# Cross attention of a decoder block on one core: context rows and value-output matrix in high and low parts, the mean row multiplied once per batch

## What is computed

```python
n_q, n_kv = 256, 120
mask = (arange(n_kv)[None, :] % n_q) == arange(n_q)[:, None]   # key j only for query j
sim = where(mask, q @ k.T * scale, -max_float)
out = softmax(sim) @ v
x = layernorm(x + out @ Wout + bout)
```

## Time and profile before

| what | before |
|---|---|
| median of three runs | 1065.95 us |
| the profiled execution | 1066.43 us |
| its span in the trace | 1064.4 us |
| TensorE (PE) busy | 983.4 us, 92% |
| VectorE (DVE) busy | 673.8 us, 63% |
| ScalarE (ACT) busy | 561.9 us, 53% |
| GpSimd (POOL) busy | 481.3 us, 45% |
| TensorE's granted clock, mean | 0.978 of full |

### The profile page before, as it was taken

One profiled execution on the slowest core, in us unless ns is written; L12 is line 12 of the kernel. 1 busy time (PEld: TensorE's weight loads), 2 busy tenths in 40 slices (PEclk: granted clock), 3 DMA queues, 4 the chain that ended last, 5 costly groups with the idle time before them and its releaser, 6 DMA issues.

```text
span 1064.4 us, 22474 instructions
## 1 busy us (share of the span) xinstructions
PE 983.4 (92%) x8461; PEld 840.3 (79%) x8461; DVE 673.8 (63%) x1454; ACT 561.9 (53%) x1338; POOL 481.3 (45%) x378
## 2 busy tenths in 40 slices
PE   3587999999999999999999999999999989989997
PEld 3465888888878888887888888888887759887887
DVE  2547676676867667686776768676432766657543
ACT  1426675766666576666657666665624433335210
POOL 7216455527835552784455278452416220006441
PEclk9668999999999999999999999999999999999999
DMA  6201000000300000030000002001135563640001
GB/s 189 81 1 40 2 12 6 2 17 1 120 4 6 11 2 16 2 120 3 2 16 2 16 2 80 2 6 42 29 98 141 148 158 93 145 99 1 20 20 41
DMA packets 71547, 47.71 MB, mean 45 GB/s; under 512 B 44464, under 2 KB 68112, under 8 KB 71440
## 3 DMA queue, kind: packets, MB, share of 16 engines
q1 hardware_dynamic: 71439, 46.27, 15.9%
HBM read 44.16 MB, written 2.10 MB: 43 GB/s over the span
## 4 chain that ended last, share of the span: by engine, by line
PE 73%; DVE 8%; SPq 8%; issue 5%; ACT 3%; POOL 2%; DMA 1%; POOLq 0%; DVEq 0%; ACTq 0%
PE F L1238 17%; PE F L1098 15%; PE A L1098 15%; PE A L1483 4%; PE A L1185 4%; PE A L1143 3%; PE A L1111 2%; SPq L298 2%; PE A L1202 2%; PE F L1111 2%; ACT prob L919 2%; SPq L306 1%; SPq L308 1%; PE A L1138 1%; PE A L1456 1%
## 5 line engine op out<-in xcount | busy, mean ns | idle before, releaser
L1098 PE MATMUL F<-xt,w 128*128 128x512 f32 x864 | 219.8, 403 | 4.6 <-ACT scratch L1081 3.9
L1098 PEld LDWEIGHTS F<-xt,w 128*128 128x128 f32 x864 | 158.8, 189 | 45.8 <-ACT scratch L1081 7.0
L385 POOL TENSOR_TENSOR ht<-scratch,ht 128x512 fp32r<-128x512 f32 x128 | 173.1, 1368 | 45.4 <-ACT ht L951 42.9
L1238 PE MATMUL F<-w,ht 128*128 128x256 f32 x1536 | 189.3, 282 | 2.0 <-POOL ht L385 2.0
L1238 PEld LDWEIGHTS F<-w,ht 128*128 128x128 f32 x1536 | 182.7, 188 | 7.8 <-issue 4.6
L374 POOL TENSOR_TENSOR rstd<-var,minus_half 128x4 f32<-128x4 f32 x32 | 37.6, 1174 | 225.4 <-DVE var L501 225.4
L948 ACT ACTIVATE scratch<-F,b_now 128x512 f32<-128x512 f32 x128 | 87.7, 685 | 44.4 <-PE F L1098 29.4
L1098 PE MATMUL A<-wa,xt 128*128 128x512 f32 x384 | 94.4, 402 | 3.5 <-issue 3.2
L1098 PEld LDWEIGHTS A<-wa,xt 128*128 128x128 f32 x384 | 72.4, 192 | 20.6 <-issue 3.6
L380 POOL TENSOR_TENSOR x<-x,vec_f 128x1024 f32<-128x1024 f32 x16 | 37.9, 2369 | 105.1 <-DVE scratch L514 105.1
L951 ACT ACTIVATE ht<-scratch 128x512 fp32r<-128x512 f32 x128 | 80.9, 632 | 4.1
(11 more groups left out here) (204 smaller groups left out, 2010.9 us busy)
## 6 DMA issues: line engine op xcount, KB each, us to landing
raw_f<-in_L_attn_W_dram SPq DMA_DIRECT2D x8, 1024.0 KB, 5.6
scratch<-in_L_ffn_fc_B_dram SPq DMA_DIRECT2D x32, 256.0 KB, 3.6
scratch<-in_L_ffn_fc_A_dram SPq DMA_DIRECT2D x32, 256.0 KB, 3.5
x<-in_x_dram SPq DMA_DIRECT2D x4, 512.0 KB, 7.4
raw_f<-in_L_ffn_fc_A_dram SPq DMA_DIRECT2D x32, 64.0 KB, 2.4
scratch<-in_x_dram SPq DMA_DIRECT2D x1, 2048.0 KB, 9.2
raw_f<-in_L_ffn_fc_B_dram SPq DMA_DIRECT2D x32, 64.0 KB, 3.0
out_dram<-x SPq DMA_DIRECT2D x3, 512.0 KB, 2.9
```

Source lines behind the costliest of these rows:

```text
L385: pool.tensor_tensor(ht[:, 1, m, :], hf[:, m % 2, :], ht[:, 0, m, :].bitcast(F32), ALU.subtract).then_inc(h_lo, 1)
L1098: last = pe.matmul(out, lhs(a, c), rhs(b, c), start=k == 0, stop=k == len(total) - 1)
L1238: last = pe.matmul(F[:, t % 2, 0:D], ht[:, a, c, P * t:P * t + P], w2[:, b, c, :], start=k == 0, stop=k == len(passes) - 1)
```

## The change

The two operands of the cross attention become pairs of float32r parts, and the product is made by three passes of float32r matmuls where it was one float32 matmul.

* **Value-output matrix.** ScalarE writes `wvo_part[0]` (float32r, in the idle buffer `ht_odd`) and then `wvo` as before, for both halves; VectorE writes the low part `wvo_part[1]`.
* **Context rows.** ScalarE writes the high part of the four groups (into idle parts of `wa` and `wo`), VectorE the low part, and VectorE reduces each group straight from PSUM: four reductions of 480 elements in place of four copies and one reduction of 1920. Then the 16 sums are scaled, ScalarE writes the high part of the eight mean columns and VectorE the low part. All of this lies in the last `step`, ahead of VectorE's y adds 2 and 3 and of ScalarE's rounding for the next MLP.
* **Mean row.** Behind the last y tile TensorE makes one 8-row product, sums of context times value-output in float32 (2 matmuls, 8 rows x 256 columns). VectorE zeroes two 128 x 256 float32r rows-tiles ahead of its last y adds, ScalarE copies the identity as float32r (`pick`), waits for the product and writes its high part, VectorE its low part. ScalarE does this ahead of pair 2 of `compose(0)`, VectorE ahead of its wait for t_sum.
* **Cross attention unit.** 6 float32r matmuls of 256 columns for the left half; 2 for the right half, where column u of `pick`, broadcast to 128 columns, picks row u of the mean rows. Before: 4 float32 matmuls of 256 columns.
* SyncE no longer waits for wvo_psum ahead of its load of x (it still waits for ctxt_psum, which TensorE signals later).

```diff
@@ -87,7 +87,6 @@
         ctx_raw = scratch[0:NKV, 0:2048].rearrange("p (b n) -> p b n", b=B)
         wvt = scratch[:, 2048:4096].rearrange("p (j i) -> p j i", j=FC)
         wout_raw = raw_a[:, :, :].rearrange("p c n -> p (c n)").rearrange("p (j n) -> p j n", j=FC)
-        ctxt = raw_a[:, :, :].rearrange("p c (b t) -> p c b t", b=B)
         wv_raw = raw_f[:, :].rearrange("p (c n) -> p c n", c=DC)
         big_raw = scratch[:, 4096:8192].rearrange("p (r n) -> p r n", r=4)
         small_raw = raw_f[:, 1024:2048].rearrange("p (r n) -> p r n", r=4)
@@ -126,6 +125,11 @@
         small = [[kt[:, i, D * r:D * r + D] for i in range(2)] for r in range(2)]
         wa_flat = wa[:, :, :, :].rearrange("p i c n -> p (i c n)")
         wo_flat = wo[:, :, :, :].rearrange("p i c n -> p (i c n)")
+        ctx_rows = [[flat.rearrange("p (b t) -> p b t", b=B) for flat in parts] for parts in (
+            (wa_flat[:, 0:1024], wa_flat[:, 1024:2048]), (wa_flat[:, 2048:3072], wo_flat[:, 0:1024]))]
+        wvo_part = [[ht_odd[:, i, D * c:D * c + D] for c in range(DC)] for i in range(2)]
+        mean_row = [xt[1][:, i, 0, 0:D] for i in range(2)]
+        pick = xt[1][:, 0, 1, 0:P]
 
         def f_ht(p, i, m):
 
@@ -183,9 +187,12 @@
         small_loaded = [sem(f"small_loaded{r}") for r in range(4)]
         t_sum, t_stats, t_mv, t_var, t_rstd, t_norm, t_bout = (
             sem(n) for n in ("t_sum", "t_stats", "t_mv", "t_var", "t_rstd", "t_norm", "t_bout"))
-        wvt_psum, wvt_out, wvo_psum, wvo_out, ctxt_psum, ctxt_out, ctx_sum, ctxt_ready, cross_psum, cross_added = (
-            sem(n) for n in ("wvt_psum", "wvt_out", "wvo_psum", "wvo_out", "ctxt_psum", "ctxt_out", "ctx_sum",
-                             "ctxt_ready", "cross_psum", "cross_added"))
+        wvt_psum, wvt_out, wvo_psum, wvo_out, ctxt_psum, ctxt_hi, ctx_sum, cross_psum, cross_added = (
+            sem(n) for n in ("wvt_psum", "wvt_out", "wvo_psum", "wvo_out", "ctxt_psum", "ctxt_hi", "ctx_sum",
+                             "cross_psum", "cross_added"))
+        wvo_lo, ctxt_lo, ctx_mean_ready, mean_hi, mean_lo, mean_zero, pick_ready, mean_psum, mean_row_hi, mean_row_lo = (
+            sem(n) for n in ("wvo_lo", "ctxt_lo", "ctx_mean_ready", "mean_hi", "mean_lo", "mean_zero",
+                             "pick_ready", "mean_psum", "mean_row_hi", "mean_row_lo"))
         at_psum, big_hi, big_lo, small_hi, small_lo, pair_done, comp_hi, comp_lo = (
             sem(n) for n in ("at_psum", "big_hi", "big_lo", "small_hi", "small_lo", "pair_done", "comp_hi", "comp_lo"))
         f_xt_psum, f_xt_hi, f_xt_lo, f_h_psum, f_gelu, f_h_hi, f_h_lo, f_y_psum, f_res = (
@@ -312,7 +319,6 @@
                 if r == 2:
                     sp.wait_ge(xt_psum[1], 8 * DEPTH)
                 load_pair(0, r, r, r, True)
-            sp.wait_ge(wvo_psum, 2)
             sp.wait_ge(ctxt_psum, 4)
             sp.dma_start(x0, x_in.rearrange("b (s p) d -> p (b s) d", p=P)).then_inc(x0_loaded, 16)
             with sp.Fori(1, PAIRS // 4) as i:
@@ -700,20 +706,35 @@
 
             def context():
 
-                dve.wait_ge(wvo_psum, 2)
+                for c in range(DC):
+                    dve.wait_ge(wvo_out, c + 1)
+                    lo(dve, wvo_part[1][c], A[:, 4 + c, 0:D], wvo_part[0][c]).then_inc(wvo_lo, 1)
                 for c in range(DC):
                     for s in range(2):
-                        dve.wait_ge(ctxt_psum, 2 * c + s + 1)
-                        dve.tensor_copy(ctxt[:, c, 4 * s:4 * s + 4, 0:NKV],
-                                        A[:, 2 * c + s, :].rearrange("p (b t) -> p b t", b=4)[:, :, 0:NKV]).then_inc(ctxt_out, 1)
-                dve.wait_ge(ctxt_out, 4)
-                dve.tensor_reduce(ctx_mean[:, :, :], ctxt[:, :, :, 0:NKV], AX_X, ALU.add).then_inc(ctx_sum, 1)
-                dve.wait_ge(ctx_sum, 1)
+                        rows = A[:, 2 * c + s, :].rearrange("p (b t) -> p b t", b=4)[:, :, 0:NKV]
+                        part = [ctx_rows[i][c][:, 4 * s:4 * s + 4, 0:NKV] for i in range(2)]
+                        dve.wait_ge(ctxt_hi, 2 * c + s + 1)
+                        lo(dve, part[1], rows, part[0]).then_inc(ctxt_lo, 1)
+                        dve.tensor_reduce(ctx_mean[:, c, 4 * s:4 * s + 4], rows, AX_X, ALU.add).then_inc(ctx_sum, 1)
+                dve.wait_ge(ctx_sum, 4)
+                dve.tensor_scalar(ctx_mean[:, :, :], ctx_mean[:, :, :], 1.0 / NKV, None, ALU.mult).then_inc(ctx_mean_ready, 1)
+                dve.wait_ge(ctx_mean_ready, 1)
                 for c in range(DC):
-                    last = dve.tensor_scalar(ctxt[:, c, :, NKV:CB],
-                                             ctx_mean[:, c, :].rearrange("p (b o) -> p b o", o=1).broadcast_to([P, B, CB - NKV]),
-                                             1.0 / NKV, None, ALU.mult)
-                last.then_inc(ctxt_ready, 1)
+                    part = [ctx_rows[i][c][:, :, NKV:CB] for i in range(2)]
+                    dve.wait_ge(mean_hi, c + 1)
+                    lo(dve, part[1], ctx_mean[:, c, :].rearrange("p (b o) -> p b o", o=1).broadcast_to([P, B, CB - NKV]),
+                       part[0]).then_inc(mean_lo, 1)
+
+            def mean_rows():
+
+                dve.wait_ge(h_psum, FC * ITEMS * DEPTH)
+                for i in range(2):
+                    dve.memset(mean_row[i].bitcast(F32), 0.0).then_inc(mean_zero, 1)
+
+            def mean_rows_lo():
+                dve.wait_ge(mean_zero, 2)
+                dve.wait_ge(mean_row_hi, 1)
+                lo(dve, mean_row[1][0:B, :], F[0:B, 0, 0:D], mean_row[0][0:B, :]).then_inc(mean_row_lo, 1)
 
             def pair_lo(f, kk, j):
 
@@ -817,8 +838,10 @@
             step(DEPTH - 1, 2)
             step(DEPTH - 1, 3, nxt=False)
             step(DEPTH - 1, 4, attn=False, nxt=False)
+            mean_rows()
             for t in range(TILES):
                 dve_res2(dve, ITEMS * DEPTH - 1, ITEMS - 1, t)
+            mean_rows_lo()
 
 
             dve.wait_ge(t_sum, ITEMS)
@@ -1001,7 +1024,19 @@
                                        A[:, WVT_BANKS[k], :], ACT.Copy).then_inc(wvt_out, 1)
                     for c in range(DC):
                         act.wait_ge(wvo_psum, c + 1)
+                        act.activation(wvo_part[0][c], A[:, 4 + c, 0:D], ACT.Copy)
                         act.activation(wvo[:, c, :], A[:, 4 + c, 0:D], ACT.Copy).then_inc(wvo_out, 1)
+                    for c in range(DC):
+                        for s in range(2):
+                            act.wait_ge(ctxt_psum, 2 * c + s + 1)
+                            act.activation(ctx_rows[0][c][:, 4 * s:4 * s + 4, 0:NKV],
+                                           A[:, 2 * c + s, :].rearrange("p (b t) -> p b t", b=4)[:, :, 0:NKV],
+                                           ACT.Copy).then_inc(ctxt_hi, 1)
+                    act.wait_ge(ctx_mean_ready, 1)
+                    for c in range(DC):
+                        act.activation(ctx_rows[0][c][:, :, NKV:CB],
+                                       ctx_mean[:, c, :].rearrange("p (b o) -> p b o", o=1).broadcast_to([P, B, CB - NKV]),
+                                       ACT.Copy).then_inc(mean_hi, 1)
                 if mlp:
                     act_xt_hi(act, 1, n - 1)
                 if attn:
@@ -1047,6 +1082,11 @@
             step(DEPTH - 1, 2)
             step(DEPTH - 1, 3, nxt=False)
             step(DEPTH - 1, 4, attn=False, nxt=False)
+            act.wait_ge(h_psum, FC * ITEMS * DEPTH)
+            act.activation(pick, ident[:, :], ACT.Copy).then_inc(pick_ready, 1)
+            act.wait_ge(mean_zero, 2)
+            act.wait_ge(mean_psum, 1)
+            act.activation(mean_row[0][0:B, :], F[0:B, 0, 0:D], ACT.Copy).then_inc(mean_row_hi, 1)
 
             with act.Fori(0, ITEMS - 1) as i:
                 for j in range(4):
@@ -1423,7 +1463,7 @@
             step(DEPTH - 1, 2)
             step(DEPTH - 1, 3, nxt=False)
             step(DEPTH - 1, 4, attn=False, nxt=False)
-            pe.wait_ge(ctxt_out, 4)
+            pe.wait_ge(ctx_sum, 4)
             multiply(0, 0, 0, True, False)
             for t in range(TILES):
                 pe_y(pe, ITEMS * DEPTH - 1, t, DEPTH - 1)
@@ -1439,22 +1479,29 @@
                     last.then_inc(f_xt_psum, 1)
 
 
+            pe.wait_ge(ctx_mean_ready, 1)
+            pe.wait_ge(wvo_out, 2)
+            pe.wait_ge(res2, RES2_0 + 16 * DEPTH - 1)
+            for c in range(DC):
+                last = pe.matmul(F[0:B, 0, 0:D], ctx_mean[:, c, :], wvo[:, c, :], start=c == 0, stop=c == DC - 1)
+            last.then_inc(mean_psum, 1)
             turn(0, 2, 2)
             multiply(0, 1, 1, False, False)
             compose(0)
             pe.wait_ge(pair_done, PAIRS)
-            pe.wait_ge(ctxt_ready, 1)
-            pe.wait_ge(wvo_out, 2)
+            pe.wait_ge(wvo_lo, 2)
+            pe.wait_ge(mean_lo, 2)
+            pe.wait_ge(mean_row_lo, 1)
+            pe.wait_ge(pick_ready, 1)
```

(9 more changed lines are left out.)

## The result

The changed kernel ran in 1060.28 us (median of 4 runs, 1059.22 to 1060.78), the kernel before in 1066.16 us beside it (4 runs, 1065.66 to 1067.10). The profiled execution took 1060.78 us, its span is 1059.2 us, 5.2 us shorter than before.

The account below looks back on a forecast made before the run. TensorE was taken to bound the kernel, busy 983.4 of 1064.4 us. From 1065.95 us, -3.8 (cross attention) + 0.1 (last step) + 0.1 (handovers) = -3.6 gave 1062.3 us; 8 in 10 range 1060.7 to 1064.3.

Parts of the forecast that it names:

- Cross attention: Stretch of eight units, 0.98 us each, the last three behind VectorE's fourth composed part: 3.8 us shorter, bounds 2.8 to 4.5.
- It passes on: Behind the cross attention: the rest depends on SyncE's queue restart or on TensorE, so all 3.8 us reach the end.
- Last step: VectorE's extra 1.5 us before y add 3 fit its 1.60 us idle; cost taken 0.1 us, bounds 0 to 0.8.
- Start of composition: ScalarE, held for the mean product, scales pair 2 0.4 us before VectorE needs it; cost 0, bounds 0 to 0.6.
- Sum: Whole kernel: -3.8 cross attention, +0.1 last step, +0.1 handovers, so -3.6 us from 1065.95.
- The range: Whole kernel: 8 in 10 for 1060.7 to 1064.3 us, from moved clock loss below to thin cover above.
- clock rival: Final MLP: an earlier arrival can spare the lower clock's 1.64 us loss, giving 1060.7 us; chance 10%.
- thin cover: Last step and ScalarE's hold at pair 2: spare too small, 1.1 and 0.6 us lost, 1063.9 us; chance 15%.
- VectorE's slow rate: Last step: the eight operations on 480 elements take 11.0 instead of 4.6 us, giving 1068.5 us; chance 5%.
- The clock in the cross attention: TensorE's 0.7 us idles there drop the clock, units 5 to 7 add 2.9 us, giving 1065.3 us; chance 5%.

Follow-up runs that it names:

- experiment 6: Changed kernel with VectorE's low parts of the second composition's pair 0 moved behind add 3; TensorE multiplying that pair earlier 1059.50 us, TensorE's order unchanged 1058.01 us.
- experiment 7: Changed kernel with the PSUM banks of the last three cross-attention units reordered, 1059.08 us; the same with experiment 6's early low parts and TensorE's order unchanged, 1057.79 us.
- Experiment 5: Changed kernel with the 8-row mean product made three times over, 1062.40 us; separately, with three more reductions in VectorE's context chain, 1062.98 us.
- the kernel's copy: The kernel before, unchanged, run against itself: 1064.43 us median of 12 runs, ratio 0.9989.

## Why the prediction was wrong in size and right in mechanism

**Cross attention: right, 0.25 us too small.** A unit was forecast at 0.98 us and ran at 0.95, or 1.04 behind a wait (882.62 to 883.66 to 884.61). The end was forecast 11.0 us behind the first matmul (887.6 - 876.6), and the last add ended 886.45 - 875.69 = 10.76 us behind it. The mis-sized term is the pace of VectorE's composed parts. The step read it as VectorE's own, 1.70 us; it was 1.58 us once TensorE was quicker (4.73 us for three periods). In the kernel before, what looked like VectorE's pace was partly TensorE's, whose units came 1.76 us apart. The adds show it: add 1 starts at 880.33 us, and adds 2 to 7 follow 1.80, 1.66, 1.79, 1.66, 1.80 and 1.65 us apart. The last four wait for TensorE, and the earlier ones keep the same rhythm, although only one of them shows an idle (add 2, then add 3):

```profile
882.13 0.69 DVE L836 TENSOR_TENSOR x<-A,x 128x512 f32<-128x512 f32 x1 [0.15 <-PE A L1456]
...
883.79 0.69 DVE L836 TENSOR_TENSOR x<-A,x 128x512 f32<-128x512 f32 x1
```

**It passes on: right.** SyncE's queue restarted 4.05 us earlier behind the first matmul, and 4.05 us became 4.2 by the end of the second composition. That it depends on this queue is shown by experiment 6, though by half of the size that I expected there, and by the lower clock in experiment 7 that cost nothing in the end.

**Last step: right.** Forecast 0.1 us of spare ahead of y add 3, measured 0.22; cost taken 0.1 us, measured 0. Experiment 5 shows that the cost behind the spare is one for one.

**Start of composition: right.** Forecast 0.4 us of spare for ScalarE, measured 0.6 by the end of its scaling; cost 0, measured 0.01 over the whole stretch, which can be told to about 0.3 us.

**Sum: the forecast should have been 4.1 us.** Its terms were 3.8, less 0.1 and 0.1; they measured 4.05 (4.2 by the end of the second composition), 0 and 0. This is the first part of the miss, 0.6 us.

**Where the sum started: the step that failed.** The prediction subtracted from 1065.95 us, the median of three runs within 0.7 us, as if that were the kernel's time. The 63 runs of the kernel before have a mean of 1065.45 us, spread from 1061.73 to 1068.18. That is the second part, 0.5 us. The changed kernel's mean over 17 runs is 1060.31 us, 2.0 us under the forecast of 1062.35; 0.9 us of these are left, the part that no trace places, and its cause stays open.

**The range failed with it.** It held a clock rival and a thin cover, but no term for the scatter of runs. With a standard deviation of 1.59 us a mean of four has a standard error of 0.8 us, and the difference of two such means 1.1 us. The measured median is no unlucky draw of the changed kernel, whose mean is the same. What was luck is the comparison: the four runs beside it have a mean of 1066.27 us, 0.8 above that of all 63, and so 5.9 us were measured where all runs give 5.1. Half a microsecond less at the start alone would have put the lower end at 1060.2, just under the result.

**The clock rival** was there (1060.7 us, the final MLP's loss spared) and was mis-sized. It took 1.64 us, the slow group's 7.40 less its twin's 5.76. In the kernel's copy the same group takes 6.22 us with a granted clock of 1.00 throughout (1025.96 to 1032.20), so only 1.2 us are the clock's, and 0.46 are not. The rival came to 1061.1 us and not 1060.7. It did not occur either: in all three profiles of the changed kernel the slow group took 7.39 to 7.41 us. Beside the final MLP, 0.80 in the first 100 us was to be read and was not, and there lies the larger part of the scatter, 4 us between the earliest and the latest of the 13 executions at about 90 us.

**The rivals.** VectorE's slow rate didn't appear: 0.56 us between operations on 480 elements. The covers held. The clock in the cross attention stayed at 1.00 with idles of 0.34 to 0.37 us in each of three periods, which is half of the idle that the rival assumed. The rival's event occurred in experiment 7, behind an idle of 2.11 us, and was hidden there. The rule from the Trainium skill (TensorE: Matmul & The Clock Gate, Back-to-back issue gap), 109 ns for an isolated matmul of 256 columns, would give 0.87 us for a unit, an estimate; the trace has 0.95 us, 119 ns for each matmul, so the row of 122 ns was the better guide.

## What to carry to other kernels

Where two engines alternate over the same banks, the period that a profile shows for one may be the other's: before a pace is used as fixed, check it against the other engine's period. Split a change in two before paying for both halves: here one repeated product was nine tenths of what the cross attention gained in the traces, and the splitting into high and low parts the rest. A starting value is a measurement too: a range needs a term for the scatter of runs, and three close runs don't give it. Here each of the places where executions of one program parted by over 0.5 us had a granted clock under 1.00 in one of them.

## What was not expected of the hardware

Two executions of the same program differ by 3.1 us on one core, 1.96 us of it before the value-output product at 773 us and 1.11 us in the final MLP, with clocks of 0.80 and 0.83, and 0.97 and 1.00, in the windows concerned. Two executions of the changed kernel part by another 1.6 us at 305 us, with clocks of 1.00 and 0.83.

The place in the final MLP is a group of 24 matmuls of 512 columns. Of the 13 executions profiled here 7 had 7.39 to 7.42 us and 6 had 6.20 to 6.22, the same program both (the kernel before 7.40, its copy 6.22), with the same idle of 1.96 or 1.97 us ahead of it. So it is not the edit that decides, nor the length of the idle. In the kernel before, the granted clock inside the slow one is 0.50 from 1029 to 1032 us; in its copy it is 1.00 all through, and the group still takes 0.46 us more than its twin's 5.76. What decides between the two, and what the 0.46 us are, no run here shows.
